# Two-layer gated cross-attention on one core: probabilities and norms 1 and 3 turned by transfers, and a new order of the stages

## What is computed

```python
x = x + tanh(g_xattn[0]) * L0_xattn(layernorm(x), ctx, ctx)   # relu(q k^T)/16 + mask, times v, relu      stage a
x = x + tanh(g_ffn[0])   * L0_ffn(layernorm(x))               # 256 -> 1024 -> 1024 -> 256, weights +-1    stage b
x = x + tanh(g_xattn[1]) * L1_xattn(layernorm(x), ctx)        # argmax rows of ctx, 16 heads, softmax      stage c
x = x + tanh(g_ffn[1])   * L1_ffn(layernorm(x))               # shared part (stage d) + top-8 of 64 experts
```

## Time and profile before

| | us |
|---|---|
| median of 3 runs (1717.62 to 1719.2) | 1718.01 |
| the profiled execution: span from first to last instruction | 1753.8 |
| TensorE busy in that span | 1618.4 (92%) |
| VectorE, ScalarE, GpSimd busy | 1345.8, 1049.5, 1023.1 |
| a usual pass between 215 and 1437 us | 44.9 |

### The profile page before, as it was taken

One profiled execution on the slowest core, in us unless ns is written; L12 is line 12 of the kernel. 1 busy time (PEld: TensorE's weight loads), 2 busy tenths in 40 slices (PEclk: granted clock), 3 DMA queues, 4 the chain that ended last, 5 costly groups with the idle time before them and its releaser, 6 DMA issues.

```text
span 1753.8 us, 51499 instructions
## 1 busy us (share of the span) xinstructions
PE 1618.4 (92%) x16676; PEld 1417.6 (81%) x16676; DVE 1345.8 (77%) x4739; ACT 1049.5 (60%) x2917; POOL 1023.1 (58%) x1664
## 2 busy tenths in 40 slices
PE   5799999999999999999999999999999997578885
PEld 3688888888888888888888888888888886367774
DVE  6488888888788888888888888888888875546554
ACT  3466666666666666666666666666666654334442
POOL 4124666666566666666666666666666654455544
PEclk8899999999999999999999999999999998689998
DMA  7502211121111111111111111111111122258886
GB/s 225 170 22 65 59 55 52 55 58 46 34 37 36 45 33 52 37 28 38 41 37 37 37 33 33 33 34 37 29 37 33 31 63 78 94 126 204 188 198 126
DMA packets 146627, 117.41 MB, mean 67 GB/s; under 512 B 74656, under 2 KB 136042, under 8 KB 146585
## 3 DMA queue, kind: packets, MB, share of 16 engines
q1 hardware_dynamic: 112792, 97.71, 19.8%
q0 software_dynamic: 33792, 19.17, 6.2%
HBM read 51.63 MB, written 111.84 MB: 93 GB/s over the span
## 4 chain that ended last, share of the span: by engine, by line
PE 73%; DMA 9%; issue 6%; ACT 5%; DVE 4%; POOL 3%; another core or an unknown queue 1%; POOLq 0%; SPq 0%; ACTq 0%; DVEq 0%
PE bank L1189 21%; DMA out<-ey,aid 9%; PE bank L1087 9%; PE bank L1173 7%; PE ps_yo L1205 5%; PE ps_yo L1087 4%; PE ps_m L1087 4%; PE ps_lg L1087 4%; ACT p L890 3%; PE ps_tr L1113 3%; PE ps_yo L1262 2%; PE ps_m L1285 2%; PE ps_pt L1262 2%; PE ps_pt L1087 2%; PE ps_lg L1249 2%
## 5 line engine op out<-in xcount | busy, mean ns | idle before, releaser
L647 POOL DMA_INDIRECT table<-xs,slot x496 | 505.3, 1019 | 188.7 <-issue 168.6
L890 ACT ACTIVATE p<-ps_lg,rmax 128x77 f32<-128x77 f32 x1024 | 251.6, 347 | 78.9 <-DVE rmax L1745 78.3
L1189 PE MATMUL bank<-h_h,held 128*128 128x256 f16 x2048 | 266.6, 273 | 2.1 <-DVE h_l L1677 1.9
L1189 PE MATMUL bank<-h_l,held 128*128 128x256 f16 x2048 | 266.3, 273 | 0.0
L602 POOL TENSOR_TENSOR pool_pad<-pad_in 128x1 f32<-128x1 f32 x418 | 90.4, 216 | 284.2 <-PE ps_tr L1294 116.8
L1189 PEld LDWEIGHTS bank<-h_l,held 128*128 128x128 f16 x2048 | 200.8, 98 | 23.6
L1189 PEld LDWEIGHTS bank<-h_h,held 128*128 128x128 f16 x2048 | 195.3, 98 | 24.3 <-issue 1.8
L1677 DVE SCALAR_TENSOR_TENSOR h_l<-bank,h_h 128x512 f16<-128x512 f32 x256 | 173.0, 685 | 32.2 <-ACT h_h L867 13.8
L690 POOL TENSOR_TENSOR rs<-nt,minushalf 128x2 f32<-128x2 f32 x128 | 93.2, 728 | 126.1 <-DVE nt L1639 115.2
L867 ACT ACTIVATE h_h<-bank 128x512 f16<-128x512 f32 x128 | 77.1, 602 | 130.3 <-PE bank L1189 127.1
L784 POOL DMA_INDIRECT out<-ey,aid x64 | 98.6, 1541 | 96.7 <-DVE aid L2031 64.1
(11 more groups left out here) (275 smaller groups left out, 4520.2 us busy)
## 6 DMA issues: line engine op xcount, KB each, us to landing
ew<-in_e_wts SPq DMA_DIRECT2D x48, 384.0 KB
table<-xg SPq DMA_DIRECT2D x8, 1284.0 KB, 17.8
xg<-table SPq DMA_DIRECT2D x64, 160.5 KB
xs<-xr SPq DMA_DIRECT2D x31, 320.0 KB
x<-in_x SPq DMA_DIRECT2D x32, 256.0 KB
out<-x SPq DMA_DIRECT2D x32, 256.0 KB
table<-xs,slot POOLq DMA_INDIRECT x496
held<-in_e_wts SPq DMA_DIRECT2D x16, 384.0 KB
```

The lines of the kernel that those rows point to most:

```text
L647: return g.indirect_dma_start(out=table, out_offset=bass.IndirectOffsetOnAxis(ap=slots[:, t, k:k + 1], axis=0), in_=rows[:, t, :], in_offs ...
L890: ins = a.activation(p32[r % 2][:, h * S2:(h + 1) * S2], ps_lg[:, g_, h % HB * S2:(h % HB + 1) * S2], ACT.Exp, bias=rmax[r % 2][:, h:h + 1])
L1189: ins = mm(two(bank[j % 2])[:, m % 2, :], wb1[:, k, m * P:(m + 1) * P], hp[:, k, :], start=(i == 0 and k == 0), stop=(i == 1 and k == FK - 1))
```

## The change

Twenty-eight of the 36 TensorE transposes of a batch go: the 20 of the probabilities, the 4 of norm 1 and the 4 of norm 3. Norm 2 and `att` stay on TensorE (`across`), in other banks. For the others, ScalarE and VectorE make the fp16 pair from the rows in SBUF, before turning, and SyncE turns the pair in one transfer: 8 blocks of 128x128 for a norm, 10 for a round of probabilities.

```diff
+            def turn(i, b):
+                made = b + 1
+                free = {1: [(l0_rdy.sem, l0_rdy.nth(3, b - 1))], 2: [(qp_rdy, b)],
+                        3: [(rt_rdy, b), (gu_rdy.sem, gu_rdy.nth(3, b - 1))], 4: [(wc_rdy, b)]}[i]
...
+                sp.wait_ge(lo_ok[i], made)
...
+                sp.dma_start_transpose(xt[i][:, :, :, :, :].rearrange("p a t c n -> p (a t c) n"),
+                                       rows_hl[i][:, :, :, :].rearrange("p a t d -> p (a t d)")).then_inc(turned[i], 16)
+            def turn_p(r, b):
+                made = p_lo.nth(r, b)
+                free = av_rdy.nth(r - 2, b) if r > 1 else av_rdy.nth(r + 2, b - 1)
...
+                sp.dma_start_transpose(pt[r % 2][:, :, :, :].rearrange("p a k n -> p (a k) n"),
+                                       p_hl[r % 2][:, :, :].rearrange("p a n -> p (a n)")).then_inc(pt_in[r % 2], 16)
...
+            def c_phi(r, b):
+                act.wait_ge(p_ok.sem, p_ok.nth(2 * r + 1, b))
+                act.wait_ge(pt_in[r % 2], pt_landed(r - 2, b))
+                a.activation(p_hl[r % 2][:, 0, :], p32[r % 2][:, :], ACT.Copy).then_inc(p_hi.sem, 1)
...
+            def c_plo(r, b):
+                dve.wait_ge(p_hi.sem, p_hi.nth(r, b))
+                v.tensor_tensor(p_hl[r % 2][:, 1, :], p32[r % 2][:, :], p_hl[r % 2][:, 0, :], ALU.subtract).then_inc(p_lo.sem, 1)
...
             def c_av(r, b):
-                pe.wait_ge(pt_lo_ok.sem, pt_lo_ok.nth(2 * r, b))
-                pe.wait_ge(pt_lo_ok.sem, pt_lo_ok.nth(2 * r + 1, b))
+                pe.wait_ge(pt_in[r % 2], pt_landed(r, b))
...
             def b_l2(t, b):
-                    w(pe, pt_lo_ok.sem, pt_lo_ok.nth(7, b - 1))
+                    w(pe, x4_ok, b - 1)
```

```diff
-            for k in range(0, E, E // 8):
-                clear_table(range(k, k + E // 8))
...
+            body(0)
+            for k in range(0, 2):
+                clear_table(range(k * step, (k + 1) * step))
+            body(1)
+            for k in range(2, 5):
+                clear_table(range(k * step, (k + 1) * step))
+            body(2)
+            for k in range(5, 8):
+                clear_table(range(k * step, (k + 1) * step))
+            body(3)
+            with sp.Fori(4, NB - 2) as n:
+                body(n)
...
+            body(2)
             pool.wait_ge(table_dma, 16 * 11)
-            body(2)
-            with pool.Fori(3, NB - 1) as n:
+            body(3)
+            with pool.Fori(4, NB - 1) as n:
```

More of the change, by code:

```diff
@@ L62, in w, with known @@
     eng.wait_ge(sem, value)
+def known(eng, *values):
+    for value in values:
+        if not isinstance(value, int):
+            eng.to_reg(value)
 class Many:
@@ L465, in clear_table, with body @@
                              xg[1][:, :].unsqueeze(1).to_broadcast([P, len(es), TW])).then_inc(table_dma, 16)
+            def body(n):
+                p, m, c, d, e = n + 2, n + 1, n - 1, n - 2, n - 3
+                if on(e):
+                    pass_rows(e)
+                if on(m) and not early(m):
+                    load_x(m)
+                if on(d):
+                    turn_p(2, d)
+                if on(n) and past(n):
+                    turn(1, n)
+                if on(d):
+                    turn_p(3, d)
+                if on(c):
+                    stack(c)
+                if on(d):
+                    turn(3, d)
+                if on(m) and not early(m):
+                    turn_x(m)
+                if on(p) and not early(p):
+                    load_ctx(p)
+                if on(e):
+                    store_x4(e)
+                if on(c):
+                    turn_p(0, c)
+                    turn_p(1, c)
             sp.wait_ge(bools_ok, 1)
@@ L470, in _ @@
             load_x(1)
+            turn(1, 0)
             sp.wait_ge(bools_ok, 2)
             load_split(8)
-            for k in range(0, E, E // 8):
-                clear_table(range(k, k + E // 8))
[L475 to L487, removed]
-            load_x(4)
-            with sp.Fori(3, NB - 2) as n:
-                stack(n - 1)
-                store_x4(n - 2, n + 1)
-                turn_x(n + 1)
-                pass_rows(n - 2)
-                load_ctx(n + 2)
-                load_x(n + 2)
+            step = E // 8
+            body(0)
[10 more added lines that the diff above has]
+                body(n)
             def load_weights(e, u):
@@ L685, in keep_x1, with keep_x2 @@
                 g.tensor_copy(x1_kept[:, :, :], x1[:, :, :]).then_inc(x1_copied, 1)
+            def keep_x2(b):
+                pool.wait_ge(x2_ok, b + 1)
+                w(pool, x3_ok, b)
+                if not isinstance(b, int):
+                    plain(3)
+                g.tensor_copy(x2_kept[:, :, :], x2[:, :, :]).then_inc(x2_copied, 1)
             def ln_coef(i, b):
@@ L963, in first @@
                 if on(c):
[L964 to L981 removed]
+                    c_exp(1, c)
@@ L1407, in first @@
[L1407 to L1421 removed]
+                    transposes(m)
                 if on(m):
[L1423 removed]
@@ L1858, in first @@
                 if on(n):
                     b_l0(0, n)
+                if on(c):
+                    ln_shift(2, c)
                 if on(d):
-                    d_ac(1, d)
+                    c_norm(3, d)
+                if on(n):
+                    b_l0(1, n)
+                if on(d):
+                    low(4, d, att[:, :, :])
+                if on(c):
+                    low(2, c, xn[2][:, :, :])
+                if on(n):
+                    b_l0(2, n)
+                    b_l0(3, n)
```

1059 lines of the change are left out of this document (522 added, 537 removed).

## The result

The changed kernel takes 1734.3 us (median of four runs, 1733.3 to 1736.9) against 1718.0 before: 1.0091 of the time, with a 95% interval of 1.0079 to 1.0104. It is 16 us slower; 53 us less had been forecast. TensorE is busy 89% of a span of 1732.6 us, where the earlier trace rows have 92% of 1753.8.

A forecast was written before the change was run, and what follows sets the result against it. The bound was to move from TensorE to a TensorE-VectorE ring of 43.0 us a pass: 60 us won in 27 passes, 7 lost at the start, 0 at the end; 1718.0 - 53 = 1665 us, range 1612 to 1735.

The forecast's parts named there:

- The ring: Steady pass, from the end of `b_l2` through TensorE and VectorE to the next `b_l2`: 43.0 us, setting the pass.
- the start: First passes: three clears behind batch 0, last three behind batch 1, GpSimd's pass 3 waiting: +7 us, between 0 and +15.
- the end: Last batches: less TensorE work and a shorter last pass against four to six uncovered turns: 0, give or take 8.
- The gain in the passes: Batches 3 to 30: 27 passes fall from 45.23 to 43.0 us, 60 us won.
- the base: Profiled 1753.8 us and its 45.23 us passes as starting point; the 35.8 us difference to the unprofiled median carried over.
- an idle time of GpSimd: GpSimd before the root of norm 2: an idle time costs 0.6 us there instead of 2; put at nothing.
- TensorE's floor: TensorE's work in a pass without 28 transposes, 3.05 us a batch: 41.8 us, 41.2 at the lowest.
- the 4.2: Landing time in us of a 10-block turn of probabilities, estimated in proportion of the blocks; bounds 3.1 and 17.8.
- The rival of late transfers: Turns landing beyond 4.2 us lengthen the ring; at 7 us the pass is 45.8, 1740 us in all; chance 0.19.
- The prediction's own sign for clears that cost more: Start: a count of batch 3 later than 230 us would show that the clears cost more.

The follow-up runs named there:

- VectorE's ring out of the way: Changed kernel with its clears ahead of the first pass, VectorE's four low parts of the gated product left out: 0.9918 of the kernel before.
- the run with more work for VectorE: Changed kernel with its clears ahead of the first pass, each of four low parts of the gated product made twice: 1.0227 of the kernel before.
- the run with another end of SyncE's list: Changed kernel with its clears ahead of the first pass, expert weight loads and last output store moved in SyncE's list: 0.9932 of the kernel before.
- the clears in front: Changed kernel with its eight clears in one block ahead of the first pass: 1708.1 us, 0.9944 of the kernel before.
- the run with the new order: The three edits, plus stage b's next first product ahead of third-round values and norm 2 statistics ahead of the third division: 0.9896 of the kernel before.
- the three edits: Changed kernel with clears ahead of the first pass, first loads not waiting for GpSimd's constants, and SyncE's list end reordered: 1697.6 us, 0.9893 of before.
- the second profile: The kernel before, unchanged, profiled a second time: ratio 1.000, span 1717.9 us.

## Why the prediction was wrong

The ring that it named held. The steps that failed are the two terms beside it: the start, put at +7 us and measured at +31, and the end, put at 0 and measured at +23. They turned a gain into a loss. The gain in the passes, put at 60 us, came out at 39: by the base, and for a good part, as far as the traces tell, by an idle time of GpSimd that was put at nothing.

**The base.** "I carry the difference over" was wrong: the 35.8 us were a property of that one execution. 9.6 of them lay in the 27 passes and were counted as if the change could win them; most others lay in the end, 10 of them in the expert loop.

**TensorE's floor: too low by 1.2.** 3.05 us of transposes left, and the floor was put at 41.2 to 41.8. With VectorE's ring out of the way it is 42.67, 1.8 under the true 44.47. What failed here is that nothing takes the place of the transposes. In the steady passes of the changed kernel TensorE has these waits (250 to 1370 us, 26 passes):

```profile
PE bank L1251 <- DVE h_l L1723: 8.4, 19, 0.6
PE ps_m L1356 <- DMA pt<-p_hl: 6.3, 7, 1.4
PE ps_m L1189 <- DVE att L1806: 4.0, 3, 1.7
```

18.7 us, 0.72 a pass, where before had 4.6 in all. The first row is `b_l0(2)`, which waits until its bank is read out. The remaining half microsecond stands in gaps too short for a row and stays open.

**The ring: right, by less than it claimed.** 43.0 were forecast, 42.80 to 42.9 measured; VectorE from `d_choose` to `d_x4` takes 1031.53 to 1047.58, 16.05 for 16.7. But in the steady pass no row shows `b_l2` waiting for `x4`, and VectorE still idles for 4.6 us a pass (under 3.5 forecast): the ring and TensorE's list came out equal. So the 42.80 alone would not show the ring; the run with more work for VectorE does.

**GpSimd's idle time: put at nothing.** Beside the 9.6 us of the base, the loop fell short of its 60 us by 11. The walk of one pass had no long passes, while the 45.23 that it was set against has them. The prediction took it that the new order hides all but 0.6 us of an idle time as in the earlier trace rows. In the changed kernel it stands in the passes behind batches 8, 15, 22 and 29 (GpSimd timeline, behind batch 15):

```profile
792.55 0.98 POOL L723 DMA_INDIRECT table<-xs,slot  x1 [3.85 <-issue]
```

The root of norm 2 stands behind it in GpSimd's list, at 796.1 us. These four passes take 44.4, 46.3, 44.0 and 49.5 us, 12.9 over four usual ones; in the kernel before the same four are 11.0 over. In the last of them some 3 us are the loads ahead of the turns, by the run with another end of SyncE's list. That the idle time makes the others long is read from the traces. Five passes behind batch 3 and one behind batch 13, of 43.1 to 43.8 us, add the rest.

**Durations: right or too long.** A low part of probabilities takes 0.83 us (0.81 forecast). Rounds issue in 1.35 us and land in 3.4 (1.66 and 4.2 forecast; ten eighths of the 3.5 would have been 4.4); a turn of 8 blocks lands in 3.0. Tiles `pt` and `rows_hl`, issue in ns and landing in us:

```profile
L470 SPq DMA_TRANSPOSE pt<-p_hl x128: 1253/1349/5919, 100.7 to 1488.2; - x128
...
DMA to landing us min/median/max: 3.3/3.4/10.1
```
```profile
DMA to landing us min/median/max: 3.0/3.0/3.5
```

The Trainium skill (Advanced Engine Details and Errata, X-Bar Transpose (TRN2)) expects transposes as fast as plain copies, at 350 to 400 GB/s, by which the prediction had estimated 0.7 us less than its 4.2. The trace's 3.4 lies at that estimate, but not at that rate: the 64 KB by which a round is larger than a norm cost 0.4 us, some 160 GB/s by estimate, nearer the 203 of the earlier trace rows.

What was wrong with the 4.2 is the proportion: by the same rows some 1.4 of the 3.0 us (an estimate) don't grow with the blocks. The rival of late transfers did not come true in the steady passes, but for 6.3 us in seven waits of `c_av` (the row above). Its 1740 us lies near the result by accident; its mechanism shows only beside the clears and at the end.

**The start: +31 for +7.** Three terms. The first loads now wait for GpSimd's constants, 6.1 us by the row above, 5.2 at the count of batch 3: a wait that stands in the diff (`sp.wait_ge(consts2, 32)` in `load_x` and `load_ctx`) and that the prediction passed over. The clears: 17.6 us at the count of batch 3, 26 in the time. The mechanism was the one named, GpSimd's pass 3 waiting for the last block, but the block went out at 157 us and the wait ended at 172, not at 136 and 150, as the first passes were late already; and GpSimd waits 26.7 us. The prediction's sum had 5 to 8 us lost by the second block, 10 by the third, and what the first passes win without 28 us of clears; by the counts it is 5.4 and 14.8 lost and only 2.8 won. What is left is 8 us with the clears in front and no wait for constants (8.5 in the run with the new order, 2.9 in the fastest execution of the three edits). No run takes it apart. TensorE's longest waits up to 95 us in the trace without that wait are for the turns of norm 1 of the first two batches, where the kernel before waited 7.9 us for the normed rows:

```profile
PE bank L1248 <- DMA xt<-rows_hl: 16.1, 2, 10.0
```

The prediction's own sign for clears that cost more, a count of batch 3 later than 230 us, came true.

**The end: +23 for 0.** The prediction set "four to six turns that nothing covers" against a shorter last pass. What it did not price is how long one batch stays in the pipeline. Count of batch 31 and output rows `x4` of the same batch, before and after:

```profile
1468.18 0.24 PE L1230 MATMUL ps_tr<-hot,ones 128*128 128x77 f16 x2
...
1514.12 0.88 DVE L1848 SCALAR_TENSOR_TENSOR x<-ps_yo,sgc,x 128x256 f32<-128x256 f32 x2
```
```profile
1463.53 0.25 PE L1313 MATMUL ps_tr<-hot,ones 128*128 128x77 f16 x2 [2.41 <-DVE hot L1761]
...
1526.69 0.88 DVE L1902 SCALAR_TENSOR_TENSOR x<-ps_yo,sgc,x 128x256 f32<-128x256 f32 x2
```

45.9 us before, 63.2 after. While the loop runs, the passes overlap and are no longer for it; behind the last batch all of it is on the path. TensorE works 34.0 instead of 26.8 us of the stretch up to the first expert's rows, since most of stage d of batch 30 now stands there, and it waits for transfers, the first two of which used to be its own transposes (1416 to 1533 us):

```profile
PE ps_tr L1165 <- DMA xt<-rows_hl: 9.3, 1, 9.3
PE ps_m L1356 <- DMA pt<-p_hl: 6.8, 2, 5.4
...
PE ps_tr L1540 <- DMA xg<-table: 4.3, 1, 4.3
```

The first of them is norm 3 of the last batch with its turn; before, TensorE waited 4.0 us there for the normed rows and 1.4 for their pair. The last is the load of the first expert's rows behind the store of the output; with the store moved it was still 4.1 us, so the store was not what cost it. The wait for the turn of norm 3 stays at 9.3 us in that run too, and that for a turn of the probabilities falls from 5.4 to 2.3. That the remaining 15 us are the longer way of the last batch is read from the traces; no run took it away.

## What to carry to other kernels

Price a new order of a pipeline in three places: the steady pass, the first passes and the way of the last batch from its last common step to its output; here 39 us were won in the first and 54 lost in the other two. Every transfer that is moved brings its waits with it, and a block of long transfers must be asked who waits for its landing, at the time at which it will then be issued. Compare the span of the profiled execution with the unprofiled times before subtracting anything from it, and take a second profile where they differ.

## What the runs showed of the hardware

Taking work from TensorE made the kernel slower: with 3.5 us less for it a pass, a wait opened, the granted clock fell to 0.73 in the 4.5 us behind it, and the pass grew from 42.8 to 44.4. Where another ring is as long as TensorE's list, work taken from TensorE alone wins nothing here.

The six added turns of a batch make many small packets. The page of the changed kernel has 382151 in all, 310175 of them under 512 bytes; that of before has 146627 and 74656. The DMA share of a pass rises from 0.14, or 0.19 in the second profile, to 0.37; the hardware queue is busy 38.4% of the span, 19.8% before.
